# Two halves of a key stack issued back to back in one DMA queue, with three other transfers and two scalings moved around them

## What is computed

```python
def _L0_xattn_ref(x, context, ...):          # x 128x512, context 12544x512, 16 heads of 32
    ctx_img, ctx_txt = context[:, :257], context[:, 257:]
    q = rms_norm(linear(x, q_w, q_b), norm_q_w)
    k = rms_norm(linear(ctx_txt, k_w, k_b), norm_k_w)
    v = linear(ctx_txt, v_w, v_b)
    ...
    return linear(attention(q, k, v) + attention(q, k_img, v_img), o_w, o_b)
...
def _mxfp4_matmul(x, codes, scales, block_size=32):
    w = codes * jnp.repeat(scales, block_size, axis=0)
    return x @ w
```

## Time and profile before

| | us |
|---|---|
| median of 3 runs | 1210.06 |
| the three runs | 1205.07, 1210.06, 1210.54 |
| profiled execution | 1210.86 |
| its span in the trace | 1209.1 |
| busy: PE, DVE, ACT, POOL | 1157.8, 946.5, 871.3, 758.3 |

### The profile page before, as it was taken

How to read it: one execution, slowest core, us unless ns; L and a number is a source line. 1 busy time by engine, 2 the same in 40 slices (tenths; PEclk the granted TensorE clock), 3 DMA queues, 4 the chain that set the end, 5 groups by cost and what they waited for, 6 DMA issues and landing times.

```text
span 1209.1 us, 26329 instructions
## 1 busy us (share of the span) xinstructions
PE 1157.8 (96%) x8794; PEld 952.2 (79%) x8794; DVE 946.5 (78%) x1611; ACT 871.3 (72%) x1891; POOL 758.3 (63%) x1064
## 2 busy tenths in 40 slices
PE   6999999999999999999999999999998789899998
PEld 4778888888888888888888888888877558588886
DVE  4777777887788778787777888778877769499997
ACT  5577777777777777777777777777777647378885
POOL 7987887888788888888888888887873000000000
PEclk9999999999999999999999999999999879999999
DMA  7135776557765668755677656676554999479990
GB/s 257 38 85 153 203 192 164 159 161 200 193 177 171 159 176 216 189 158 149 179 204 193 165 162 168 188 203 171 167 142 102 281 393 392 159 250 364 367 362 22
DMA packets 129327, 236.72 MB, mean 196 GB/s; under 512 B 15014, under 2 KB 42150, under 8 KB 128812
## 3 DMA queue, kind: packets, MB, share of 16 engines
q1 hardware_dynamic: 129196, 235.05, 65.4%
HBM read 140.87 MB, written 17.04 MB: 131 GB/s over the span
## 4 chain that ended last, share of the span: by engine, by line
PE 69%; SPq 13%; DMA 5%; POOL 5%; DVE 4%; issue 3%; ACT 2%; ACTq 0%; POOLq 0%; DVEq 0%
PE ps L1571 25%; PE ps L1435 14%; SPq L354 11%; PE ps L1597 5%; DMA k_stack<-kt_hi 5%; PE ps L1630 5%; PE ps L1798 3%; PE ps L1801 3%; PE ps L1804 3%; PE ps L1819 1%; PE ps L1827 1%; DVE small L1195 1%; PE ps L1823 1%; PE ps L1775 1%; POOL cx_blocks L621 1%
## 5 line engine op out<-in xcount | busy, mean ns | idle before, releaser
L1571 PE MATMUL ps<-w_text,cx_blocks 128*128 128x512 f32 x1974 | 488.4, 394 | 0.5 <-ACT v_first L812 0.5
L1571 PEld LDWEIGHTS ps<-w_text,cx_blocks 128*128 128x128 f32 x1974 | 366.9, 188 | 86.8 <-issue 9.4
L855 ACT ACTIVATE p<-ps,small 128x512 f32<-128x512 f32 (+2 forms) x400 | 272.4, 683 | 85.4 <-DVE small L1197 80.2
L1195 DVE TENSOR_REDUCE small<-ps 128x1 f32<-128x512 f32 (+2 forms) x400 | 269.5, 674 | 62.8 <-PE ps L1597 61.9
L1435 PE MATMUL ps<-ident,p 128*128 128x128 f32 x1584 | 213.4, 274 | 24.6 <-ACT p L855 14.4
L1435 PEld LDWEIGHTS ps<-ident,p 128*128 128x128 f32 x1584 | 184.8, 141 | 59.0 <-ACT p L855 22.2
L837 ACT ACTIVATE pt<-ps 128x512 f32<-128x512 f32 (+1 forms) x296 | 164.5, 592 | 22.0 <-PE ps L1435 21.9
L621 POOL TENSOR_TENSOR cx_blocks<-cx_sum,small 128x256 fp32r<-128x256 f32 x188 | 122.7, 653 | 58.5 <-PE ps L1571 46.8
L1197 DVE TENSOR_TENSOR small<-small 128x1 f32<-128x1 f32 x400 | 139.3, 348 | 13.7
L623 POOL TENSOR_TENSOR cx_blocks<-cx_sum,cx_blocks 128x256 fp32r<-128x256 f32 x188 | 140.4, 747 | 14.8
L1597 PE MATMUL ps<-k_stack,q_stack 96*128 96x512 f32 (+1 forms) x400 | 145.6, 440 | 0.0
(11 more groups left out here) (252 smaller groups left out, 1964.1 us busy)
## 6 DMA issues: line engine op xcount, KB each, us to landing
expert<-experts SPq DMA_DIRECT2D x34, 1536.0 KB, 8.9
k_stack<-kt_hi SPq DMA_DIRECT2D x384, 128.0 KB, 3.0
cx<-ctx_t SPq DMA_DIRECT2D x48, 512.0 KB, 4.5
k_stack<-kt_lo SPq DMA_DIRECT2D x192, 128.0 KB, 2.9
codes<-codes SPq DMA_DIRECT2D x64, 256.0 KB, 4.5
code_scale<-code_scales SPq DMA_DIRECT2D x64, 256.0 KB, 4.8
scaled<-codes SPq DMA_DIRECT2D x64, 256.0 KB, 4.4
weight_q<-scaled SPq DMA_DIRECT2D x1, 4096.0 KB, 14.1
```

Of the source, the lines that this page charges most:

```text
L855: eng.activation(pb[:, lo:hi], score_bank(s, h)[:, lo:hi], exp, bias=nm[1 - par][:, h:h + 1], accum_out=ls[1 - par][:, h:h + 1]).then_inc( ...
L1195: eng.tensor_reduce(ngm[:, h:h + 1], score_bank(s, h)[:, lo:hi], AX.X, ALU.max, negate=True).then_inc(e_gm, 1)
L1571: last = eng.matmul(ps_a[(p + i + 1) % 2][:, :], blk[:, i, a, c * P:(c + 1) * P], w_t[:, i, w, c * D:(c + 1) * D], start=(i in FRESH and c ...
```

## The change

The stack's half 0 and, in the next step, its half 1 stand directly behind each other in SP's stream. For that, pass 2 of the codes moves from the end of a step to behind half 1 and the second context half of the next step, and `load_next` moves from behind half 0 to ahead of it, between pass 1 and the wait for the keys. On GpSimd the first two scalings of a step move later: the one that stood ahead of `split_first(0)` goes behind the split of block 3, and the one that stood behind the fourth sum goes behind the split of block 6. No instruction is added or removed.

```diff
                 if nxt and (loop or s > 0):
                     eng.wait_ge(e_ab, s * (2 * NPOS))
                     load(s + 1, 1)
+                if s > 0:
+                    pass_codes(s - 1, 2, (s - 1) % UNROLL, loop)
                 pass_codes(s, 0, m, loop)
...
                 pass_codes(s, 1, m, loop)
                 if 1 <= s < NG:
+                    load_next(s)
                     eng.wait_ge(e_klo, s * GT + GT)
                     if score:
                         eng.wait_ge(e_qk, s * NH - NH // 2)
                     stack(0, False)
-                    load_next(s)
...
-                pass_codes(s, 2, m, loop)
...
-                scale_codes(s * W_STEP - (W_FIRST * W_STEP + 1), (m + 1) % 2, loop)
                 if strass:
                     split_first(0)
...
                     split(0, 3, sum_x[:, :, :], 0)
+                scale_codes(s * W_STEP - (W_FIRST * W_STEP + 1), (m + 1) % 2, loop)
+                if strass:
                     third_sum(0)
                     split(0, 4, sum_x[:, :, :], 3)
                     fourth_sum(0)
-                scale_codes(s * W_STEP - W_FIRST * W_STEP, m % 2, loop)
...
                     split(0, 6, quarter(0, 1, 1), 0)
+                scale_codes(s * W_STEP - W_FIRST * W_STEP, m % 2, loop)
```

## The result

The changed kernel takes 1201.62 us in the median of 7 runs (1197.79 to 1207.84), the kernel before 1210.06 (7 runs beside them, 1205.07 to 1211.43). The ratio is 0.9946 [0.9925, 0.9968]: faster by 8 us, where 18 to 19 were forecast. The time lies in the range, the gain is less than half of the forecast. The ratios in this document leave out two slow executions, one of 1450.45 us of the kernel with pass 2 moved (granted clock 0.75) and one of 1214.51 us of the kernel before.

The account below looks back on a forecast made before the run. TensorE was taken to bound the kernel, with gaps from ScalarE's wait for the key stack. 18.5 us over 21 steps plus 0.3 ahead, 18.8, from 1210.9 gave 1192.1, stated as 1192; range 1188 to 1204.

Parts of the forecast that it names:

- What bounds the kernel: TensorE, 96% busy, loses 0.88 us a step to gaps because ScalarE's exponentials wait for the key stack's last transfer.
- What TensorE absorbs: ScalarE's wait for the stack that leaves TensorE without a gap: between 1.0 and 2.0 us, taken as 1.5.
- The floor of 36.36 us a step: TensorE's own time for a step without the loss, against 37.24 us a step in the kernel before.
- The stack, half 1: Half 1 starts 2.2 us earlier, ScalarE waits nothing to 1.0 us, TensorE loses nothing: gain 21 x 0.88 = 18.5 us.
- The context half, earlier: `load_next` issued 9 to 12 us sooner gives GpSimd slack, saves nothing by itself; cost nothing, cover about 4 us.
- The three passes: Passes 2, 0, 1 in a row behind half 1 add waits for scales, but half 0 is not delayed and GpSimd loses nothing.
- The margin of half 0: SP's queue is ready for half 0 1.0 us before the last low keys that half 0 must await.
- ring: Rival 4: SP's queue becomes a loop longer than TensorE's step, 38.2 us, so 20 us slower, 1231; chance 0.07.
- The lock between VectorE and GpSimd: GpSimd's scalings hold VectorE's small minimum, 0.62 us instead of 0.16; moved scalings hold other heads' minima.
- The second rival: Minima held by moved scalings become late, 0.46 us a step on TensorE, 9.7 us back: about 1202; chance 0.11.
- That the landing would not come forward: Rival 3: the DMA engines, not the issue, set when the stack lands, so about 1210; chance 0.06.
- if the `ot_sb` rows keep a spacing over 36.8: Sign of a wrong forecast: TensorE's `ot_sb` transposes, once a step, stay over 36.8 us apart; 36.4 was expected.

Follow-up runs that it names:

- pass 2 moved: Changed kernel with pass 2 of the codes issued ahead of the second context half, not behind it: 1192.99 us, ratio 0.9904; again 1196.07 us, 0.9901.
- the light scalings: Changed kernel with pass 2 issued ahead of the second context half and only 8 of 512 columns of the codes scaled: 1187.56 us, ratio 0.9838.
- both edits together: Changed kernel with the last key norm ahead of the first two sums and pass 2 ahead of the second context half: 1189.67 us, 0.9846; again 1189.06 us, 0.9857.
- second profile: The changed kernel, nothing altered, timed again beside later variants against the kernel before: 1200.72 us, ratio 0.9949.
- the norm moved: Changed kernel with GpSimd's last key norm moved ahead of the first two sums of the second context half: 1193.45 us, ratio 0.9914.
- the fill: Changed kernel with pass 2 ahead of the second context half and each scaling replaced by a 0.95 us write-only GpSimd fill: 1197.5 us, ratio 0.9925.

## Why the time fell in the range and the gain was less than half

**What bounds the kernel.** Right. The wait for the stack was the gap before the transposes: with 50.1 of its 53.7 us gone, so are 12.7 of the 14.4 us of TensorE's waits for exponentials, all of them in the 21 steps. What TensorE absorbs was taken a little low, 1.5 us: in the kernel before a wait of 1.71 us (at 511.53) leaves no gap and one of 1.97 us (at 475.04) a gap of 0.17, and the longest, 3.79, one of 1.75, so it is about 2.0 us in most steps. The floor of 36.36 us a step was right to 0.01 us (the light scalings). So the gain of 0.88 us a step was there to be had, and both edits together have most of it: 37.24 to 36.44 or 36.53.

**The stack, half 1.** Right: a wait between nothing and 1.0 us was expected, 3.6 us in 6 places came, the longest 1.2. How much of the gain is the earlier start and how much the 1.28 MB that no longer stand ahead is not settled: with 512 KB of them taken away alone, landings came forward by twice as much as the start, 0.8 against 0.4 us, and not by the 1.5 to 1.9 expected.

**The context half, earlier.** Right for GpSimd, whose wait for `cx` is gone from the list; wrong in "cost nothing, cover about 4 us". Half 0 is issued right behind pass 1 and the context half, and the cover is gone in some steps: a score waits for the stack once in the profile of the changed kernel (0.8 us of excess), in 3 steps of its second profile (2.3 us) and in 5 with the norm moved (5.5 us). With the context half alone ahead of half 0, and pass 1 some 9 us before, no score waits. The stack's issues take longer too: the 12 of half 0 a median of 8.7 us, 7.7 in the kernel before, and all 24 a median of 16.5 and 17.98 in the long step, where I took 15.3. That puts the scales of pass 2 later than I had them. The forecast put the first scaling's start at 437.6, 20.5 us after that step's `ot_sb` row (417.06); it came 21.5 to 24.2 us after.

**The three passes.** The margin of half 0 was read rightly on the whole: it starts within 1.0 us of the last low keys (1.5 in the second profile), and no ring was formed. In 5 of the 21 steps it does start straight behind the context half, the sign that was named for a ring. The step that failed is the sentence "GpSimd gives up nothing for it: same instructions, fewer waits", with "its lead over TensorE (some 10 us) covers", said of the third scaling, behind it. The lead is one of the blocks it splits. The norm of the last key tile has no such lead: its squares come from ScalarE in the middle of the step, and ScalarE uses it at once. The first scaling was moved to a place ahead of it, and scales that land late hold the whole stream there. I named that norm in the walk through the second scaling, and took its time from the row of before, 446.44, as fixed. I did not ask who waits for it. The true lead of the norm can be worked out from the rows after: with the first scaling at 20.5 us into the step, as forecast, 1.3 us for it, 6.0 us of work and 0.8 for the norm it is ready at 28.6, and gaps begin behind 30.6. That is 2 us of lead and not 10, and the scaling came 1.0 to 3.7 us late. The term missing from the sum is about 7 us (0.34 a step): 7.1 us of excess in the steps with a gap at kb, some 1 us of which is the price of two score gaps in them. The timed ratios of the edits that remove the cause, 0.9914 and 0.990 against 0.995, give 4 us (norm moved) and 6 us (pass 2 moved).

**The lock between VectorE and GpSimd.** The second rival priced a held minimum that becomes late at 0.46 us; the fill measured 0.52. It came in 5 of the 21 steps of the changed kernel, not in all, and by a split and not by a scaling: some 2.6 us at that price, where the rival had 9.7. That the total ended at this rival's 1202 is chance; most of the excess, 7.1 of 10.9 us, stands in steps with a gap at kb. The Trainium skill, page "SBUF — State Buffer", section "Who interferes with whom", names as partners a VectorE instruction with two SBUF inputs and a GpSimd instruction that reads SBUF, not one that only writes. The kernel with the fills agrees, rows of VectorE and GpSimd in its timeline:

```profile
453.72 0.95 POOL L518 MEMSET codes<- 128x1024 bf16 x1 [1.74 <-DMA code_scale<-code_scales]
453.85 0.16 DVE L1199 TENSOR_TENSOR small<-small 128x1 f32<-128x1 f32 x1
...
454.63 0.61 POOL L622 TENSOR_TENSOR cx_blocks<-cx_sum,small 128x256 fp32r<-128x256 f32 x1
454.65 0.61 DVE L1199 TENSOR_TENSOR small<-small 128x1 f32<-128x1 f32 x1
```

Inside the fill the minimum takes 0.16 us, inside the split 0.61, to the split's end.

**The other rivals.** That the landing would not come forward is refuted by the 3.6 us. The ring did not close, though SP's idle time ahead of half 0 went from 7 to 10 us to between 0.1 and 1.9. Of the signs that the prediction named, the waits came as stated, and "if the `ot_sb` rows keep a spacing over 36.8" was the one that showed it wrong: 36.88. It gave the right warning and no cause.

**What stays open.** Why the first scaling's move delays the stack in the old queue; how the gain divides between an earlier start and less queued ahead; and what makes the stack land late in the few long steps when the context half alone is moved.

## What to carry to other kernels

An in-order engine has no one lead; it has one for each consumer. Before work that can wait for a transfer is put into its stream, list what stands behind it and ask of each item who uses it and when, above all of the small ones. And when the bottleneck's gap is closed, read off the list of waits which ones are short now, since those at 2 to 8 us are the next to appear.

## What the runs showed of the hardware that I had not expected

- The lock works both ways. GpSimd's scaling, 1.29 us alone, took 1.82 us from 596.25, just after VectorE had begun an instruction with two SBUF inputs:

```profile
596.24 0.68 DVE L1225 TENSOR_TENSOR o_st<-o_st,small 128x512 f32<-128x512 f32 x1
```

- A shorter instruction on an engine that is off the path can lock a bad phase: fills of 0.95 us in place of scalings of 1.29 us gave 36.87 or 36.88 us in 17 of 21 steps, whole scalings 36.55 on average.
- SP's issues take longer when much is queued ahead: 12 issues of half 0 took a median of 7.7 us in the kernel before, with nothing issued in the 7 us ahead of them, and of 8.7 us in the changed one, with 1.28 MB issued in the 5 us ahead; all 24 took from 15.4 to 18.0 us with the same instructions.
- A wait costs more than its length once the clock falls: with GpSimd's old order in the new queue TensorE's granted clock is 0.94 over the 21 steps, and its busy time 53 us longer for the same matmuls.
- Apart from that kernel, TensorE's granted clock is at the lower level for 10 to 34 us of an execution, differently from run to run of one kernel, mostly where the steps have ended. The two profiled executions of the kernel with both edits took 1196.12 and 1188.98 us; their steps differ by 1.7 us and their time at the lower level by 17.0, of which about half, 8.5, would be lost (an estimate). That is as much as this change gives, and only medians over many runs told the edits apart.
